# Spreading each g row over 64 partitions with a transfer of its own, in a state-space and expert kernel on one Trainium2 core

## What is computed

```python
proj = xn @ x_proj_w.T
delta, B_ssm, C_ssm = jnp.split(proj, [R, R + N], axis=-1)
delta = jax.nn.softplus(delta @ dt_proj_w.T + dt_proj_b)
A = -jnp.exp(A_log)
C_used = C_ssm[:, jnp.arange(L) % CHUNK, :]

def step(h, inp):
    dt, b, xt, c = inp
    dA = jnp.exp(dt[:, :, None] * A)
    h = dA * h + dt[:, :, None] * b[:, None, :] * xt[:, :, None]
    y = jnp.einsum('bdn,bn->bd', h, c)
    return (h, y)
...
return (y + x * D_param) @ out_proj_w.T
```

```python
h = jnp.einsum('th,ehi->tei', x2d, w1_experts)
a = relu2(h) * route_w[:, :, None].astype(x2d.dtype)
routed = jnp.einsum('tei,eih->th', a, w2_experts)
return (shared + routed).reshape(orig_shape)
```

## Time and profile before

| | |
|---|---|
| median of 3 runs | 1863.0 us (1857.44 to 1863.48) |
| the profiled execution | 1870.5 us, span of its instructions 1868.2 us |
| busy PE / DVE / ACT / POOL | 1031.4 / 932.9 / 577.6 / 573.8 us (55 / 50 / 31 / 31% of the span) |
| mean granted TensorE clock | 0.646 of full speed |
| DMA | 232.80 MB, mean 125 GB/s |
| main part, tiles 32 to 230 | from 331.56 us to 1693.38 us |

### The profile page before, as it was taken

How to read it: one execution, slowest core, us unless ns; L and a number is a source line. 1 busy time by engine, 2 the same in 40 slices (tenths; PEclk the granted TensorE clock), 3 DMA queues, 4 the chain that set the end, 5 groups by cost and what they waited for, 6 DMA issues and landing times. The chain is left out here.

```text
span 1868.2 us, 21312 instructions
## 1 busy us (share of the span) xinstructions
PE 1031.4 (55%) x6823; PEld 572.8 (31%) x6824; DVE 932.9 (50%) x842; ACT 577.6 (31%) x847; POOL 573.8 (31%) x391
## 2 busy tenths in 40 slices
PE   3775056465564565645655555646656556554335
PEld 3443012233332343323333223323323233331114
DVE  5796899433342343433334233333334233348994
ACT  1124533333332333423333233323323233332210
POOL 2016770222222222223223223213222222226770
PEclk8898555566666666666666576666676566765557
DMA  9903831333333333333333343333343333335332
GB/s 340 304 0 110 284 116 35 103 124 108 121 122 96 121 125 115 116 106 124 121 113 101 108 128 121 121 97 124 105 128 119 102 119 120 113 122 153 103 101 93
DMA packets 187707, 232.80 MB, mean 125 GB/s; under 512 B 48201, under 2 KB 143818, under 8 KB 187338
## 3 DMA queue, kind: packets, MB, share of 16 engines
q1 hardware_dynamic: 178378, 206.12, 34.5%
q0 software_dynamic: 9216, 25.18, 4.3%
HBM read 154.05 MB, written 77.07 MB: 124 GB/s over the span
## 5 line engine op out<-in xcount | busy, mean ns | idle before, releaser
L969 DVE TENSOR_TENSOR_SCAN H<-ps,U 128x1024 f32<-128x1024 f32 x256 | 584.9, 2286 | 252.6 <-ACT ps L700 91.1
L601 POOL TENSOR_TENSOR U<-X,B 128x1024 f32<-128x1024 f32 x100 | 234.6, 2346 | 987.4 <-DMA X<-g_d 972.8
L1133 PE MATMUL ps<-PK,sel 24*128 24x512 bf16 x824 | 242.4, 583 | 267.7 <-DVE H L969 127.0
L700 ACT ACTIVATE ps<-ps,Acur 128x1024 f32<-128x1024 f32 x256 | 279.8, 1093 | 272.6 <-PE ps L1133 272.5
L953 DVE TENSOR_TENSOR U<-ps,B 128x512 f32<-128x512 f32 x98 | 67.5, 689 | 591.8 <-PE ps L1133 591.8
L1192 PE MATMUL ps<-ident,XG 128*128 128x128 f32 x360 | 98.1, 427 | 476.4 <-DMA XG<-xg_d 476.4
L1122 PE MATMUL ps<-H,CB 128*32 128x128 f32 x4096 | 269.9, 401 | 13.6 <-DVE H L969 6.1
L724 ACT COPY XT<-ps 128x512 f32<-128x512 f32 x90 | 52.7, 586 | 606.3 <-PE ps L1192 606.3
L1192 PEld LDWEIGHTS ps<-ident,XG 128*128 128x128 f32 x360 | 63.1, 213 | 518.4 <-issue 505.3
L1133 PEld LDWEIGHTS ps<-PK,sel 24*128 24x128 bf16 x824 | 44.4, 98 | 442.3 <-issue 280.2
L1181 PE MATMUL ps<-WE,AS 128*128 128x256 f32 x360 | 179.2, 650 | 0.0
(11 more groups left out here) (146 smaller groups left out, 593.5 us busy)
## 6 DMA issues: line engine op xcount, KB each, us to landing
X<-g_d SPq DMA_DIRECT2D x100, 512.0 KB
WE<-w_exp_dram SPq DMA_DIRECT2D x184, 256.0 KB, 6.3
xg_d<-CB SPq DMA_DIRECT2D x23, 1024.0 KB, 11.1
XG<-xg_d SPq DMA_DIRECT2D x92, 256.0 KB, 13.5
yg_d<-YO SPq DMA_DIRECT2D x90, 256.0 KB, 19.4
PK<-pk_d SPq DMA_DIRECT2D x64, 128.0 KB, 10.0
pk_d<-GS SPq DMA_DIRECT2D x16, 256.0 KB, 3.5
X<-x_dram SPq DMA_DIRECT2D x4, 512.0 KB, 5.6
```

Of the source, the lines that this page charges most:

```text
L601: nc.gpsimd.tensor_tensor(U[:, c % 4, :], rows, B2[:, b * L:(b + 1) * L], ALU.mult).then_inc(u_pool, 1)
L700: nc.scalar.activation(a_tile(c), a_tile(c), ACT.Exp, scale=Acur[:, b, pair:pair + 1]).then_inc(a_ready, 1)
L969: V.tensor_tensor_scan(H[:, (s // GRP % 2) * GRP + s % GRP, :], a_tile(s), U[:, s % 4, :], 0.0, ALU.mult, ALU.add).then_inc(scan_done, 1)
L1133: return mm(ps[:, bank, :], sel[32 * g:32 * g + ROWS, c % SUB, :], PK[32 * g:32 * g + ROWS, c // SUB % NPK, :], start=True, stop=True)
```

## The change

The transfer of both rows of a pair becomes two transfers, one for each row: first that of the second row, to partitions 64 to 127, then that of the first, to partitions 0 to 63. Both add 16 to the slot's semaphore, so POOL waits for twice the count. The bytes that land are the same, 512 KB for each tile.

```diff
             def load_g(block_no, c):
 
                 b, pair = c // PAIRS % NBATCH, c % PAIRS
-                sp.dma_start(gslot[dma_slot(c)],
-                             g_d[bass.ds(block_no * CH + 2 * pair, 2), b, :].unsqueeze(1).broadcast_to((2, N, L)))\
-                    .then_inc(s_gs[dma_slot(c)], 16)
+                for d2 in (1, 0):
+                    sp.dma_start(gslot[dma_slot(c)][d2 * N:(d2 + 1) * N, :],
+                                 g_d[bass.ds(block_no * CH + 2 * pair + d2, 1), b, :].broadcast_to((N, L)))\
+                        .then_inc(s_gs[dma_slot(c)], 16)
...
                         if g_rows_dma(it, c):
-                            pool.wait_ge(s_gs[dma_slot(c)], (by_dma(it, c) - dma_slot(c)) * 16 // NGS + 16)
+                            pool.wait_ge(s_gs[dma_slot(c)], (by_dma(it, c) - dma_slot(c)) * 32 // NGS + 32)
```

## The result

The changed kernel takes **1202.7 us** (median of 4 runs, 1200.46 to 1205.16) against 1863.2 us, a ratio of 0.646 (95% interval 0.6442 to 0.6478). Forecast were 1192 us, within 1145 to 1355. The profiled execution took 1201.9 us, its span is 1199.5 us.

What follows compares the result with a forecast made beforehand. Two full DMA engines were taken to bound the main part. Loop transposes at 343 us, six blocks of 110.3 (to 1005), an end of 189.9 and 2.3 outside the span gave 1197, as a median 1192 us; range 1145 to 1355.

Steps and rivals of the forecast that it cites:

- bound before: two full DMA engines: Tiles 32 to 230: g loads and other traffic fill two DMA engines for 1240 of 1361.8 us, 91%.
- first transposes of the loop: Loop start: with free queues, faster stores and `XG` load bring PE's first transposes from 357.09 to 343 us.
- last transposes to the scan of tile 224: Last stretch of the six blocks, up to the scan's end forecast at 1005 us; put at 12 us.
- the end: Behind the scan of tile 224: 205.1 us less two g-row waits of 8.70 and 6.48, leaving 189.9 us.
- the ends of the blocks: Each of six blocks: 15 pairs with experts, plus one worth of scan alone at DVE's 5.3 us.
- The bound, and what comes last behind it: Main part: two full DMA engines bound it before; afterwards PE's own sequence, 6.65 us a pair, SP right behind.
- The allowance for pairs in the loop: Pairs in the loop: PE and SP wait for each other, so 7.0 us, halfway between 6.65 and 7.38.
- The clock: PE's granted clock over the loop, 0.64 before, taken at the upper level throughout once the waits are gone; above 0.9.
- The load: A tile's g load costs 1.24 us of all sixteen DMA engines in place of 9.9 us on two.
- The rival of a DMA bound: Loop: a g load costing four times 1.24 us makes pairs 8.8 us, up to 1354 us in all; chance 0.18.
- The low clock: Loop: clock stays low, pairs take 9.6 us, 1426 us in all; chance 0.07, shared with a load dearer still.
- The two without a gain: g loads: both halves still share two engines, 1863 us, chance 0.04; or one engine takes all, 2720 us, chance 0.06.

Runs made afterwards that it cites:

- the runs with 2, 4 and 8: Changed kernel with transfers cut by columns, both rows in each (2 engines): 1866.6 us; row's repeats listed 4 x 16: 1401.6 us; 8 x 8: 1225.6 us.
- the run with one row: Changed kernel with only the second row of each pair loaded, half of the g bytes, so its output is not right: 1200.8 us, one execution.
- the run that is cut by columns: Changed kernel with its two transfers each carrying both rows and half of the 1024 columns: 1866.6 us, 1.0006 of the kernel before.
- the run beside: The changed kernel measured again beside the run with blocks 1 to 6 written out: 1202.6 us, 0.6458 of the kernel before.

## Why the prediction was right

By its own steps, with the time of the profiled execution:

| step | forecast | measured |
|---|---|---|
| bound before: two full DMA engines | 91% of the stretch | the share itself not measured; that the load on k engines sets the time is shown by the runs with 2, 4 and 8 |
| first transposes of the loop | 343 us | 339.4 |
| 84 pairs inside the blocks | 7.0 us each | 6.81 (572 us in all) |
| 5 intervals across a block's end | 12.3 us each | 17.9 (89.3 us in all) |
| last transposes to the scan of tile 224 | 12 us | 9.0 |
| the end | 189.9 us | 189.8 |
| span | 1195 | 1199.5 |
| time of the profiled execution against the median | 0.4% above | 0.1% below |

The span comes out within 5 us because the terms miss in opposite ways: -16 us for the pairs and +28 us for the ends of the blocks, -4 and -3 for the two small ones. That closeness is luck: each of the two large terms missed by more than the sum did. The remaining 5 us between 1197 and 1202 is that same sum, and the other half of the miss of the median, 1192 against 1202.7, comes from scaling by the one execution of before.

**The bound, and what comes last behind it: right.** The step that carried the forecast was to read the share of 0.13 at 53 GB/s as two engines, and then to look for the next bound not in the busy times but in a pair that had run before the queue was full. PE's sequence of 6.65 us was taken from there, and 67 of 84 pairs run at 6.55.

**The allowance for pairs in the loop: right in size, wrong in its reason.** The step said that PE and SP, nearly equal, would wait for each other and make 6.65 into 7.0. SP works 6.67 us for a pair (658 less 31 us over 94 pairs, with the ends of the blocks in it; 6.1 to 6.3 were put down), but less work for it changed nothing. What lifts 6.55 to 6.81 is the clock, in 16 of the 17 pairs of 7.8 us. *The clock* was forecast to stay at the upper level for the whole loop, and is 0.91.

**The term that was mis-sized: the ends of the blocks.** The step gave each block "one worth of scan alone at DVE's 5.3", as if there were no loop. Written out, two pairs there take 11.6 us, 0.7 less than the sum had; as a loop they take 17.9. Nothing in the trace of before was read for it, though its rows show the interval at 17.3 to 18.5 us and, in it, two pauses of PE with no releaser.

**The load: right in its effect, wrong in its price.** 1.24 us of sixteen engines were taken, 2.1 to 2.2 are shown, by the stretch with g loads alone and by the run with one row. The step that failed in it is "at the rate of each engine now": 26.5 GB/s for each engine did not hold for sixteen. It did not matter, as the loop did not come to 1.0. The rival of a DMA bound was closer than it looked: a share of 0.7 was expected, 0.80 is there.

**The rivals.** Reading one place by sixteen engines costs nothing against reading 64 places. The low clock did not stay. The two without a gain fell with the shares of the runs: a row listed 64 times goes to sixteen engines, and a transfer with the rows listed outermost to two. The Trainium skill's rule that two transfers to disjoint partition halves bring nothing ("DMA: Bandwidth & Descriptors", "Rules for kernel authors") does not hold here, since the single transfer was not spread over sixteen engines; the run that is cut by columns is the case in which two transfers bring nothing, 1.0006.

## What to carry to other kernels

When no engine is busy and all wait for a DMA, look at the DMA share in windows of 1 to 6 us, best where one kind of load runs alone: a plateau at k/16 said here, for 2, 4, 8 and 16, that a transfer used k engines, and the outermost dimension of its patterns said why. Put a dimension that sixteen divides outermost, if need be by more transfers. Then find the next bound in a stretch where the old one did not yet hold, and look at the ends of a hardware loop, which a bound elsewhere hides.

## What the runs showed of the hardware that was not expected

- A hardware loop on all five engines costs some 6 us each time round here (17.9 us, or 17.6 in the run beside, against 11.6 written out), with up to 2.70 us of it in the middle of PE's instructions, while 4 to 6 packets of code are loaded at each end.
- Sixteen engines with nothing but g rows move 250 GB/s at a share of 1.00, 15.6 each; two move 50 GB/s, 25 each.
- SP issues a load of 64 rows of 4 KB in 0.5 us and one of 32 rows in some 0.4 us (medians of 200 and 400). In the loop before, an issue of `XG` could take 5.09 us, and two of `ys_d` took 10.90 where it began; with the load spread over sixteen engines this is gone, so it came with the two full ones.
- The granted clock falls to its lower level in single pairs while PE is busy for 553 of 600 us, and as often as when it is busy for 499.
